# A memset and a wait behind each row scatter in a two-layer attention and mixture-of-experts kernel

## The chip, the core and the metric
The kernel runs on one core of a Trainium2 chip. The metric is the device time of one execution in microseconds (us). TensorE does matrix products, VectorE (DVE in the profile) and ScalarE (ACT) elementwise work, GpSimd (POOL) some elementwise work and the DMAs whose addresses come from a table of indices, SyncE (SP) issues the other DMAs.

## What is computed
Eight sequences of 256 tokens with 256 features go through two blocks. The first has attention with 16 heads and a small feed-forward layer that picks one of 8 low-rank updates per token. The second has causal attention with 16 query heads over 4 key groups, then a mixture of 32 experts, four per token, and one shared expert. The part around the change is the last:

```python
logits = flat @ router_w.T
scores = jnp.sqrt(jax.nn.softplus(logits))
_, idx = jax.lax.top_k(scores + expert_bias, K)        # K = 4 of E = 32
...
def body(acc, xs):
    wg, wu, wd, p = xs
    return (acc + p[:, None] * _clamped_swiglu(flat, wg, wu, wd), None)
```

## The kernel before
The 2048 tokens are 16 tiles of 128, two per sequence. The second attention goes through the sequences b = 0 to 7 and in each through 16 heads (a head step is b * 16 + head). TensorE computes scores into a ring of three banks, ScalarE exponentiates them (line 1162), TensorE multiplies by the values, VectorE divides (`divide`), adds to x and takes row statistics.

When a sequence has been divided, GpSimd computes the scale of its rows (`scale_rows`, lines 917 and 918), ScalarE normalizes the rows with it (`normalize_row`, line 1100), TensorE turns them and computes the logits, VectorE picks four experts for each token (`top_four`, `pick_four`), TensorE counts ranks within the experts (`ranks`) and VectorE turns them into row numbers (`find_slots`, line 2175; semaphore `slots_ready`). This goes by batches of sequences, `BATCHES = ((0, 2), (2, 2), (4, 2), (6, 1), (7, 1))`, each a first sequence and a count.

The rows are then sorted by expert in DRAM (`rows_by_expert`, 2048 rows for each expert): GpSimd issues 64 indirect DMAs, one for each tile t and pick k (`scatter`, line 922), each of which writes 128 rows of 260 floats. Its queue is in program order:
- During sequences 4 to 7, `scatter_nth` issues the scatters of batches 0 and 1 and five of batch 2, each behind a wait for its slots and for the exponential of a given head step. In each of these sequences `scale_rows(b - 1)` stands at head 8, in the same queue.
- Behind the attention come two more scatters of batch 2, a wait for the last division, two more, `scale_rows(7)`, the last seven of batch 2, picks 3 and 2 of batch 3 (four scatters), and then twelve: picks 3 and 2 of batch 4 (the last sequence), pick 1 of batches 3 and 4, pick 0 of batches 3 and 4.

Meanwhile VectorE works out which blocks of 128 rows belong to which expert, and SyncE loads blocks (`load_block`, line 761) from `rows_by_expert` for TensorE, which turns each (line 1720) and multiplies it by its expert's weights (1731, 1742). The first eight blocks wait for levels of the semaphore `picks_placed`: a token's picks are in order of expert number, so expert 0's rows are all in pick 3 (level 1), expert 1's in picks 3 and 2 (level 2), all others need all 64 scatters (level 3, which GpSimd sends itself when `placed[0]` says that the last have landed). Expert 0 has 338 rows here (three blocks), expert 1 has 411 (four). There are 80 block steps. Results go back by rank through 80 more indirect DMAs of GpSimd (line 982).

Of the kernel before, what the change touches and what calls it, by code (L numbers as in the profile page):

```python
# [16 lines left out]
P = 128  # L17
# [10 lines left out]
QT = SEQ // P  # L28
# [13 lines left out]
TAG = 16384.0  # L42
MASKED = -1.0e30
BLOCKS = -(-(TOKENS * TOPK + EXPERTS * (P - 1)) // P)
TURNS = 8
BLOCKS += -BLOCKS % TURNS
FEWEST = TOKENS * TOPK // P // TURNS
LEADING = 2 * TILES // TURNS + 1
FIRST = 8
# [113 lines left out]
BATCHES = ((0, 2), (2, 2), (4, 2), (6, 1), (7, 1))  # L163
# [73 lines left out]
def two_block_kernel(nc, x_in, wqkv0, wproj, bproj, wffn, debias, wdown, center, slope,  # L237
                     wqkv1, bq1, bk1, bv1, router, ebias, wexp_in, out):
    ctx = ExitStack()
    with ctx:  # L240
        def sb(name, shape, dt=F32):
            return ctx.enter_context(nc.sbuf_tensor(name, shape, dt))
# [4 lines left out]
        def cut(whole, start, size, shape=None, **axes):  # L247
            part = whole[:, start:start + size]
            return part.rearrange(shape, **axes) if shape else part
# [90 lines left out]
        work = cut(exps, 0, TILES * TOPK * EXPERTS, "p (t k e) -> p t k e", t=TILES, k=TOPK)  # L340
        SMALL = ONE_AT + (EXPERTS - 2) * EW
        most = max(size for _, size in BATCHES) * QT * EXPERTS
        lg, soft, ex, ln = (cut(arena, SMALL + i * most, most, tile_expert, t=most // EXPERTS) for i in range(4))
        sbi = cut(arena, SMALL + 2 * most, most, tile_expert, t=most // EXPERTS)
# [34 lines left out]
        sco = cut(arena, PICK_F + TOPK * te, te, tile_expert, t=TILES)  # L379
        trash = cut(arena, PICK_F + TOPK * te + te, BLOCKS)  # L380
        sg, se = (cut(attn_w, i * CHUNK, CHUNK) for i in (0, 2))
# [3 lines left out]
        wsh = cut(exps, P_RING * P_WIDTH[1], EW)  # L385
        tagb, pad, valid = (cut(exps, 4 * CHUNK + i * BLOCKS, BLOCKS) for i in range(3))
        experts = cut(arena, ONE_AT, EXPERTS * EW)
# [9 lines left out]
        goes = sb("goes", [P, 4], U32)  # L397
        vec = sb("vec", [P, 12])
        zero = sb("zero", [P, XW])
        before = sb("before", [P, P], BF16)  # L400
        onesb = sb("onesb", [P, P], BF16)
        m8 = cut(ffn_w, 0, TILES * 8, "p (t e) -> p t e", t=TILES)
# [12 lines left out]
        slot = cut(bpb, 2 * EXPERTS, TILES * TOPK).bitcast(U32).rearrange("p (t k) -> p t k", t=TILES)  # L415
        eb_i = sb("eb_i", [1, BLOCKS], I32)
        start_i = sb("start_i", [1, BLOCKS], I32)
        first_i = sb("first_i", [1, 2 * FIRST], I32)
# [14 lines left out]
        xs = nc.dram_tensor("rows_by_expert", [EXPERTS * TOKENS, XW], F32, kind="Internal").ap()  # L433
        ys = nc.dram_tensor("results_by_rank", [TOKENS * TOPK + BLOCKS * P, D], F32, kind="Internal").ap()

# [112 lines left out]
        def block_trips(eng):  # L548

            eng.wait_ge(blocks_ready, 2)  # L550
            return eng.value_load(trips_i[0:1, 1:2], min_val=0, max_val=BLOCKS // TURNS - FEWEST) + FEWEST

# [81 lines left out]
        def _(sp):  # L634
# [117 lines left out]
            def starts_of(first, size):  # L752
                return nc.values_load_multi_w_load_instructions(
                    start_i[0:1, bass.ds(first, size)],
                    engines=[mybir.EngineType.SP], min_val=0, max_val=EXPERTS * TOKENS - P,
                    skip_runtime_bounds_check_because="a block's first row lies in its expert's rows")[1]
# [16 lines left out]
            trips = block_trips(sp)  # L773
            with sp.Fori(FIRST // TURNS, trips) as i:
                starts = starts_of(TURNS * i, TURNS)
                for j in range(TURNS):
# [24 lines left out]
        def _(pool):  # L801
# [29 lines left out]
            def then(ins):  # L831

                pool_steps[0] += 1
                ins.then_inc(pool_step, 1)
                pool.wait_ge(pool_step, pool_steps[0])
# [84 lines left out]
            def scatter(t, k):  # L920

                pool.indirect_dma_start(xs, bass.IndirectOffsetOnAxis(ap=slot[:, t, k:k + 1], axis=0),  # L922
                                        xn4[:, t, :], None).then_inc(placed[max(k - 1, 0)], 16)

            def scatter_nth(j, n, after):
                pool.wait_ge(slots_ready, j + 1)
                pool.wait_ge(exp_ready[1], after + 1)
                t, k = divmod(n, TOPK)
                scatter(BATCHES[j][0] * QT + t, k)

            def scatter_picks(j, picks):

                pool.wait_ge(slots_ready, j + 1)
                first, size = BATCHES[j]
                for k in picks:
                    for t in range(first * QT, (first + size) * QT):
                        scatter(t, k)
# [20 lines left out]
            for t, k in tiles[:2]:  # L958
                scatter(t, k)
# [839 lines left out]
        def _(dve):  # L1799
# [280 lines left out]
            def pair(n, b, k):  # L2080
                count = b * len(PAIRS[n]) + k
                src = pair_bank[count % 2]
                dve.wait_ge(unit_ready[n], count + 1)
                (qt, h0, nh, nk), (_, h1, _, _) = PAIRS[n][k]
                if n == 0:
                    out = mx[b % 2][:, :, h0:h0 + nh]
                    ins = dve.tensor_reduce(out, src.rearrange("p (q h k) -> p q h k", q=QT, k=nk), AX.X, ALU.max)  # L2087
                else:
                    out = mx[b % 2][:, qt, h0:h0 + 2 * nh]
                    ins = dve.tensor_reduce(out, src.rearrange("p (h k) -> p h k", k=nk), AX.X, ALU.max)  # L2090
                ins.then_inc(unit_done[n], 1)
                if k == len(PAIRS[n]) - 1:
                    dve.wait_ge(unit_done[n], count + 1)
                    if b:
                        dve.wait_ge(negT_ready[n], b)
                    step(n, dve.tensor_scalar(neg[:, :, 0, :], mx[b % 2][:, :, :], -1.0, None, ALU.mult))
                    dve.scalar_tensor_tensor(out=neg[:, :, 1, :], in0=mx[b % 2][:, :, :], scalar=-1.0, in1=neg[:, :, 0, :],
                                             op0=ALU.mult, op1=ALU.subtract).then_inc(neg_ready[n], 1)
# [335 lines left out]
```

## Time and profile before

| what | us |
|---|---|
| median of 3 runs | 607.91 |
| lowest, highest | 606.37, 610.05 |
| span of the profiled execution, first to last instruction | 624.5 |
| TensorE busy | 550.5 (88%) |
| VectorE busy | 433.0 (69%) |
| ScalarE busy | 346.5 (55%) |
| GpSimd busy | 241.2 (39%) |
| GpSimd in the 64 scatters | 63.2 |
| GpSimd idle just before them | 57.6 |

The profile is that of another execution than the timed ones. Its own device time isn't recorded apart from the span; it can only be longer than the span. The span is 16.6 us above the median. A row of the timeline gives start, duration, engine, line and operation, and in brackets the idle time of the engine before it and what ended it.

### The profile page before, as it was taken

The page shows a single profiled execution, that of the slowest core. Times are in us where ns is not written, and L with a number is a line of the kernel's source. Part 1 is how long each engine was busy: PE and PEld are TensorE (multiplying, and loading weights), DVE is VectorE, ACT ScalarE, POOL GpSimd, SP SyncE. Part 2 cuts the span into 40 slices and gives each one's busy share as a digit, 9 for nine tenths or more (in the row PEclk, how much of TensorE's full clock was granted, in tenths as well). Part 3 has the DMA queues.
Part 4 walks back from the last instruction along what each step waited for, and adds up shares of the span by engine and source line. Part 5 has one row for each costly group of instructions (what it writes and reads, how often), then busy time and mean ns, then how long its engine had stood idle before and what let it go on. Part 6 is the DMA issues. An engine that isn't in the chain of part 4 may idle for free.

```text
span 624.5 us, 14114 instructions
## 1 busy us (share of the span) xinstructions
PE 550.5 (88%) x4231; PEld 390.9 (63%) x4232; DVE 433.0 (69%) x1298; ACT 346.5 (55%) x898; POOL 241.2 (39%) x341
## 2 busy tenths in 40 slices
PE   9998799999879989989998888866589999989996
PEld 4665455665458754666666665534367787778775
DVE  5678858888147886677788683535667777778755
ACT  3533657776826578456675456513146565656672
POOL 2533000000153213266544435556735555555530
PEclk9999979999999999999999899778799999999998
DMA  8599707000680005766505162235545454445498
GB/s 252 179 304 331 211 1 207 3 3 3 192 219 1 2 1 166 209 206 183 229 19 206 62 229 71 70 137 219 170 126 140 140 159 144 151 135 154 143 396 328
DMA packets 49554, 95.24 MB, mean 153 GB/s; under 512 B 8596, under 2 KB 40540, under 8 KB 46940
## 3 DMA queue, kind: packets, MB, share of 16 engines
q1 hardware_dynamic: 41820, 75.34, 39.4%
q0 software_dynamic: 7680, 19.21, 8.2%
q8 instruction: 30, 0.49, 0.3%
q14 instruction: 24, 0.20, 0.1%
HBM read 58.54 MB, written 35.59 MB: 151 GB/s over the span
## 4 chain that ended last, share of the span: by engine, by line
PE 54%; DVE 20%; issue 9%; ACT 6%; DMA 4%; POOL 3%; another core or an unknown queue 2%; SPq 1%; DVEq 0%; ACTq 0%; POOLq 0%
PE banks L1731 7%; PE banks L1513 6%; PE banks L1469 5%; PE banks L1322 4%; PE banks L1742 4%; PE banks L1534 4%; DVE mx L2087 3%; DVE mx L2090 3%; PE banks L1399 3%; PE banks L1794 2%; PE banks L1328 2%; DMA arena<-negT 2%; PE banks L1720 2%; DMA pvs<-rows_by_expert 2%
## 5 line engine op out<-in xcount | busy, mean ns | idle before, releaser
L1162 ACT ACTIVATE arena<-banks 128x512 f32<-128x512 f32 (+1 forms) x256 | 130.1, 550 | 83.3 <-PE banks L1513 45.8
L982 POOL DMA_INDIRECT results_by_rank<-attn_w,goes x80 | 77.3, 966 | 72.2 <-issue 47.9
L1513 PE MATMUL banks<-arena 98*128 98x256 bf16 (+1 forms) x512 | 88.6, 267 | 15.9 <-DVE arena L2186 3.8
L2087 DVE TENSOR_REDUCE mx<-banks 128x4 f32<-128x1024 f32 x64 | 76.0, 1220 | 18.1 <-PE banks L1469 18.0
L922 POOL DMA_INDIRECT rows_by_expert<-arena,bpb x64 | 63.2, 987 | 57.6 <-ACT arena L1162 22.4
L1469 PE MATMUL banks<-arena 96*128 96x256 bf16 (+1 forms) x512 | 81.5, 263 | 4.2 <-DVE mx L2087 2.5
L1731 PE MATMUL banks<-arena,attn_w 128*128 x320 | 84.4, 387 | 0.3 <-issue 0.3
L1513 PEld LDWEIGHTS banks<-arena 98*128 98x128 bf16 x512 | 43.2, 100 | 49.7 <-ACT arena L1162 15.0
L2090 DVE TENSOR_REDUCE mx<-banks 128x4 f32<-128x1024 f32 (+1 forms) x48 | 57.7, 1221 | 22.3 <-PE banks L1473 20.2
L1469 PEld LDWEIGHTS banks<-arena 96*128 96x128 bf16 x512 | 49.9, 99 | 20.0 <-issue 6.0
L1731 PEld LDWEIGHTS banks<-arena,attn_w 128*128 128x128 f32 x320 | 55.6, 194 | 5.1 <-issue 0.7
L1742 PE MATMUL banks<-arena,attn_w 128*128 x160 | 49.0, 388 | 7.4 <-issue 4.1
L1235 ACT ACTIVATE attn_w<-attn_w 128x128 f32<-128x128 f32 x80 | 24.8, 310 | 53.3 <-DVE attn_w L2285 40.0
L2285 DVE TENSOR_SCALAR attn_w<-banks 128x256 f32<-128x256 f32 x80 | 34.0, 424 | 24.8 <-PE banks L1731 12.3
L848 POOL DMA_DIRECT2D arena<-negT x24 | 12.1, 509 | 99.5 <-ACT negT L1084 99.5
L1473 PE MATMUL banks<-mask_s,identb 128*128 128x128 bf16 x256 | 40.3, 221 | 0.5 <-issue 0.5
L1742 PEld LDWEIGHTS banks<-arena,attn_w 128*128 128x128 f32 x160 | 28.8, 189 | 16.5 <-issue 12.8
L1720 PE MATMUL banks<-ident,pvs 128*128 128x128 f32 x160 | 31.7, 281 | 7.7 <-DMA pvs<-rows_by_expert 7.7
L1534 PE MATMUL banks<-arena 128*17 128x256 f32 x512 | 34.7, 389 | 1.1 <-ACT pvs L1093 1.1
L944 POOL TENSOR_SCALAR_AFFINE_SELECT arena<-arena 128x256 f32<-128x256 f32 x64 | 26.0, 418 | 21.2 <-ACT arena L1162 21.1
L1241 ACT ACTIVATE attn_w<-banks 128x256 f32<-128x256 f32 x80 | 31.0, 387 | 2.8 <-DMA results_by_rank<-attn_w,goes 2.5
L840 POOL TENSOR_TENSOR arena<-arena 128x512 bf16<-128x512 f32 x16 | 18.2, 1160 | 37.1 <-ACT arena L994 37.1
(253 smaller groups left out, 1095.7 us busy)
## 6 DMA issues: line engine op xcount, KB each, us to landing
arena<-parts_dram SPq DMA_DIRECT2D x72, 256.0 KB, 4.1
pvs<-rows_by_expert SPq DMA_DIRECT2D x80, 130.0 KB
parts_dram<-arena SPq DMA_DIRECT2D x24, 384.0 KB, 4.8
arena<-results_by_rank SPq DMA_DIRECT2D x6, 1024.0 KB, 10.3
arena<-in SPq DMA_DIRECT2D x2, 2304.0 KB
rows_by_expert<-zero SPq DMA_DIRECT2D x1, 4160.0 KB, 23.6
arena<-in SPq DMA_DIRECT2D x2, 1920.0 KB
arena<-in SPq DMA_DIRECT2D x3, 768.0 KB
```

The source lines that it names most:

```text
L922: pool.indirect_dma_start(xs, bass.IndirectOffsetOnAxis(ap=slot[:, t, k:k + 1], axis=0), xn4[:, t, :], None).then_inc(placed[max(k - 1, 0) ...
L982: pool.indirect_dma_start(ys, bass.IndirectOffsetOnAxis(ap=goes[:, j % 4:j % 4 + 1], axis=0), yb[j % 4], None).then_inc(y_stored[j % 4], 16)
L1162: act.activation(p_ring[n][:, i % P_RING, :], st_bank[RING_AT[n]["s", b, s] % 3][:, 0:P_WIDTH[n]], ACT.Exp, scale=HD ** -0.5).then_inc(exp ...
L1469: ins = pe.matmul(dst[:, a * nk:(a + 1) * nk], q_rows(n, slice(0, STACK), h0 + a, b, qt * P, P), k_rows(n, slice(0, STACK), h0 + a, b, 0, ...
L1473: ins = pe.matmul(dst[:, a * nk + nk - P:(a + 1) * nk], identb[:, :], mask_s[:, :], start=False, stop=True)
L1513: ins = pe.matmul(dst[:, at:at + SEQ - q0], keys, q_rows(n, slice(0, ROWS), s, b, q0, SEQ - q0), start=True, stop=(n == 0 or b < POOL_MASKS))
L1534: ins = pe.matmul(pv_bank[rows, col:col + SEQ], vals, p[:, kt * SEQ:(kt + 1) * SEQ], start=(kt == 0), stop=(kt == QT - 1))
L1720: ins = pe.transpose(bank[p][:, k * P:(k + 1) * P], xb[:, q, k * P:(k + 1) * P], ident[:, :])
L1731: ins = pe.matmul(bank[2 + p][:, 0:2 * INNER], xbT[:, p, k, :], experts[:, bass.ds(e * EW + k * 2 * INNER, 2 * INNER)], start=(k == 0), st ...
L1742: pe.matmul(bank[6 + p][:, 0:D], hidT[:, p, :], experts[:, bass.ds(e * EW + 2 * KD * INNER, D)], start=True, stop=True).then_inc(y_ready, 1)
L2087: ins = dve.tensor_reduce(out, src.rearrange("p (q h k) -> p q h k", q=QT, k=nk), AX.X, ALU.max)
L2090: ins = dve.tensor_reduce(out, src.rearrange("p (h k) -> p h k", k=nk), AX.X, ALU.max)
```

## The change
A tile `pause` of 128x256 floats is allocated. Behind each scatter whose tile t is below 14 (all but the last sequence's), GpSimd writes zeros to it, and `then` makes GpSimd wait until that memset has finished before it goes on. 56 of the 64 scatters are followed by it. Nothing reads the tile.

```diff
+PAUSE = 256
...
+        pause = sb("pause", [P, PAUSE])
...
                 pool.indirect_dma_start(xs, bass.IndirectOffsetOnAxis(ap=slot[:, t, k:k + 1], axis=0),
                                         xn4[:, t, :], None).then_inc(placed[max(k - 1, 0)], 16)
+                if t < BATCHES[4][0] * QT:
+                    then(pool.memset(pause[:, :], 0.0))
```

GpSimd's queue from the scatters in the heads of sequence 7 to the one behind the last division, before (L917 and L918 are the scaling of rows, `divided1` the last division):

```order
L922 DMA rows_by_expert<-arena,bpb 65536x260 [waits exp_ready1,slots_ready] x5
L922 DMA rows_by_expert<-arena,bpb 65536x260 x2
L922 DMA rows_by_expert<-arena,bpb 65536x260 [waits divided1]
L922 DMA rows_by_expert<-arena,bpb 65536x260
L917 TENSOR_TENSOR rstd<-var,mhalf 128x2 [waits rows_var]
```

The same place now, from the fourth of the five on (numbers of the queue in front, lines are two or more higher):

```order
196 L924 DMA rows_by_expert<-arena,bpb 65536x260 [waits exp_ready1,slots_ready,pool_step]
197 L927 MEMSET pause 128x256
198 L924 DMA rows_by_expert<-arena,bpb 65536x260 [waits exp_ready1,slots_ready,pool_step]
199 L927 MEMSET pause 128x256
200 L924 DMA rows_by_expert<-arena,bpb 65536x260 [waits pool_step]
201 L927 MEMSET pause 128x256
202 L924 DMA rows_by_expert<-arena,bpb 65536x260 [waits pool_step]
203 L927 MEMSET pause 128x256
204 L924 DMA rows_by_expert<-arena,bpb 65536x260 [waits divided1,pool_step]
205 L927 MEMSET pause 128x256
206 L924 DMA rows_by_expert<-arena,bpb 65536x260 [waits pool_step]
207 L927 MEMSET pause 128x256
```

The order of the scatters is the same; each next one waits for `pool_step`, the memset's semaphore, and the scaling of the last rows stands behind nine memsets counted from the first of the five.

The last twelve scatters on GpSimd, before:

```order
L922 DMA rows_by_expert<-arena,bpb 65536x260 [waits slots_ready]
L922 DMA rows_by_expert<-arena,bpb 65536x260 x3
L922 DMA rows_by_expert<-arena,bpb 65536x260 [waits slots_ready]
L922 DMA rows_by_expert<-arena,bpb 65536x260
L922 DMA rows_by_expert<-arena,bpb 65536x260 [waits slots_ready]
L922 DMA rows_by_expert<-arena,bpb 65536x260
```

And now (the first row is the last sequence's first scatter):

```order
232 L924 DMA rows_by_expert<-arena,bpb 65536x260 [waits slots_ready,pool_step]
233 L924 DMA rows_by_expert<-arena,bpb 65536x260 x3
234 L924 DMA rows_by_expert<-arena,bpb 65536x260 [waits slots_ready]
235 L927 MEMSET pause 128x256
236 L924 DMA rows_by_expert<-arena,bpb 65536x260 [waits pool_step]
237 L927 MEMSET pause 128x256
238 L924 DMA rows_by_expert<-arena,bpb 65536x260 [waits slots_ready,pool_step]
239 L924 DMA rows_by_expert<-arena,bpb 65536x260
```

Two memsets stand between picks 1 of batch 3 and those of batch 4; the same pattern follows once more for pick 0, so four of the twelve are followed by one.

## Rows read from the trace of the kernel before

**Rows 1.** The page of the profile, its first line.
```profile
span 624.5 us, 14114 instructions
```

**Rows 2.** Busy us (instructions) by stretch: PE, PEld, DVE, ACT, POOL; clock, DMA share, GB/s.
```profile
400.00:425.00 25.00, 17.86 (x140) 11.43 (x139) 10.87 (x37) 9.65 (x23) 14.02 (x17) 0.86 0.41 149
425.00:450.00 25.00, 14.10 (x73) 8.34 (x72) 16.97 (x67) 4.84 (x10) 16.97 (x18) 0.80 0.51 175
...
500.00:525.00 25.00, 23.70 (x129) 19.78 (x127) 18.71 (x94) 14.67 (x57) 13.88 (x15) 1.00 0.53 154
```

**Rows 3.** Timelines of TensorE, ScalarE, TensorE, VectorE: start, us, engine, line, operation.
```profile
406.30 0.22 PE L1516 MATMUL banks<-mask_t,identb 128*128 128x128 bf16 x1
...
411.02 0.49 ACT L1162 ACTIVATE arena<-banks 128x384 f32<-128x384 f32 x1 [5.77 <-remote]
...
432.48 0.21 PE L1591 MATMUL banks<-products,onesb 128*128 128x32 bf16 x1
...
436.36 0.22 DVE L2167 SCALAR_TENSOR_TENSOR arena<-iota,banks 128x64 f32<-128x64 f32 x1 [3.63 <-remote]
```

**Rows 4.** The chain that ended last, SyncE's part: start, us, what.
```profile
443.24 0.74 SPq L747
...
444.19 0.04 SPq L768
...
445.64 0.68 SPq L761
...
454.86 0.03 SPq L768
...
455.14 2.06 DMA pvs<-rows_by_expert
```

**Rows 5.** Timeline of TensorE, the transpositions of blocks 4 and 7.
```profile
457.24 0.44 PE L1720 MATMUL banks<-ident,pvs 128*128 128x128 f32 x2 [0.44 <-DMA pvs<-rows_by_expert]
...
462.17 0.38 PE L1720 MATMUL banks<-ident,pvs 128*128 128x128 f32 x2
```

**Rows 6.** Timeline of GpSimd, 371 to 453 us: scatters (L922) and scalings.
```profile
371.41 0.96 POOL L922 DMA_INDIRECT rows_by_expert<-arena,bpb  x1 [7.80 <-DVE bpb L2175]
...
378.70 1.04 POOL L922 DMA_INDIRECT rows_by_expert<-arena,bpb  x1 [0.52 <-issue]
...
386.89 0.96 POOL L922 DMA_INDIRECT rows_by_expert<-arena,bpb  x1 [2.43 <-ACT arena L1162]
...
399.70 0.72 POOL L917 TENSOR_TENSOR rstd<-var,mhalf 128x2 f32<-128x2 f32 x1
...
402.50 1.04 POOL L922 DMA_INDIRECT rows_by_expert<-arena,bpb  x1 [1.80 <-ACT arena L1162]
...
416.90 1.28 POOL L922 DMA_INDIRECT rows_by_expert<-arena,bpb  x1 [5.80 <-DVE arena L2191]
418.49 0.96 POOL L922 DMA_INDIRECT rows_by_expert<-arena,bpb  x1 [0.31 <-issue]
419.48 0.73 POOL L917 TENSOR_TENSOR rstd<-var,mhalf 128x2 f32<-128x2 f32 x1
420.28 0.19 POOL L918 TENSOR_TENSOR shift<-nmean,rstd 128x2 f32<-128x2 f32 x1
420.64 1.04 POOL L922 DMA_INDIRECT rows_by_expert<-arena,bpb  x1 [0.16 <-issue]
...
437.98 0.96 POOL L922 DMA_INDIRECT rows_by_expert<-arena,bpb  x1 [3.15 <-DVE bpb L2175]
...
452.18 0.96 POOL L922 DMA_INDIRECT rows_by_expert<-arena,bpb  x1 [0.30 <-issue]
```

**Rows 7.** DMA activity, 454 to 455 us, in 40 slices (0.025 us each, tenths).
```profile
DMA  8440000000000000000000000000000000000000
```

**Rows 8.** Line 809, GpSimd's memset of a tile of nearly the same size.
```profile
L809 POOL MEMSET zero<- x1: 336/336/336, 1.6 to 1.6; 128x260 f32 x1
```

**Rows 9.** Timeline of ScalarE: the normalization that waits for the scaling at 399.70.
```profile
400.73 0.60 ACT L1100 ACTIVATE arena<-arena,shift,rstd 128x256 f32<-128x256 f32 x1 [0.77 <-POOL shift L918]
```

## The prediction
> **What bounds the kernel now.** I read the busy shares in windows of 25 us first, then the chain that ended last where TensorE idles, then the timelines of the engines on both sides of each idle piece. TensorE works nearly all the time in the expert loop (23.70 of 25 us), but only 17.86 and 14.10 of 25 us between 400 and 450 us [rows 2]. This stretch, from the end of the second attention to the first expert blocks, is the one that the change touches, so its chain decides.
>
> Two odd things are to be seen in it. One: TensorE starts its last score matmul at 406.30 (0.22 us), and ScalarE, idle and waiting for it, starts at 411.02; what ended its 5.77 us of idle time is given as "remote", which is nobody on this core [rows 3]. An ordinary hand-over leaves about 0.1 us, so some 4.4 us are unexplained. TensorE's rank matmul ends at 432.69, idle VectorE takes the ranks at 436.36: another 3.6 us [rows 3]. Two: behind the instruction at 444.19 SyncE's register instructions, 0.04 us each before, take about 0.68 us each; at 454.86 they are back at 0.03 [rows 4]. All of these lie where GpSimd issues scatters every 1.26 us without a break (0.96 us of work, 0.30 us between) [rows 6]. And the rate behind them: from block 4 on TensorE runs at (462.17 - 457.24) / 3 = 1.64 us a block [rows 5], so whatever delays the early blocks passes to the end unreduced.
>
> Block 7 is the first whose expert is number 2 (the inputs give experts 0 and 1 three and four blocks), and its load waits for level 3, which is all 64 scatters landed. The last scatter starts at 452.18 and the packets in the software queue end 0.1 us into the window from 454 [rows 6, 7]: 1.9 us from start to landing. From a load's start to its first transposition it is 457.24 - 455.14 = 2.1 us [rows 4, 5].
>
> **What is the profile's own.** The span is 624.5 us [rows 1], 16.6 above the median of 607.91, and what lies around a span would only add to that. The loop runs at TensorE's own rate, so the surplus isn't spread evenly; it must sit in idle time, and the unexplained idle time lies in these 50 us. Take both stalls out and let SyncE's instructions cost 0.04: all of the last batch's work comes 8.0 us earlier, and SyncE takes up the blocks at 443.24 - 8.0 = 435.2 [rows 4]. The first load goes out about 1.2 us after that (0.74 for the table and a dozen instructions at 0.04), and block 7 would be on TensorE at 436.4 + 2.1 + 7 x 1.64 = 450.0. GpSimd's side allows it: with the first stall gone (the second isn't on its way) its last twelve scatters could start at 430.7, or at 437.98 less the two stalls, 430.0, if the slots came last; the last of them starts 452.18 - 437.98 = 14.2 later, at 444.9 [rows 6], and 444.9 + 1.9 + 2.1 = 448.9. So block 7 moves from 462.17 to 450.0, and 624.5 - 12.2 = 612.3 is near the timed runs. I therefore take it as likely that timed runs don't have these stalls.
>
> That rests on rows; a page points the same way. The Trainium skill ("NOTIFIC — the notification-queue block", section 3, Interfaces) says that trace records leave through a block that can hold back the engines that write them when an internal FIFO fills. No run here shows that block. By it a pause would mend the profile and not the timed run.
>
> **The change, part by part.** It adds 56 memsets of 128x256 and 56 waits, behind each of the 64 scatters but the last sequence's 8; it removes and moves nothing else. The allocation of a tile costs no time.
> - One memset: the nearest row is the 128x260 one, 336 ns [rows 8]; I take 0.34.
> - Its wait and what follows: a GpSimd instruction behind a scatter starts after 0.03 (419.45 to 419.48), one behind its own wait after 0.07; the scatter that follows a compute instruction starts after 0.16 where it waits for nothing, 0.52 where it also names exp_ready and slots_ready, and takes 1.04 instead of 0.96 [rows 6].
> - So the spacing of scatters that are all ready goes from 1.26 to 1.04 + 0.03 + 0.34 + 0.07 + 0.52, about 2.03, in the head-by-head part, and to 1.68 in the tail. The low bound for both has the short gap and the short scatter: 0.96 + 0.03 + 0.34 + 0.08 + 0.17, about 1.60. Below that nothing is possible, since the memset can't start before the scatter ends nor the next scatter before the memset does.
>
> GpSimd is idle before many scatters, waiting for the exponential or the slots that gate them, and this hides the pauses as long as a gate comes later than the queue. It no longer does from batch 1 on. With 2.03: four scatters from 371.41, then the fifth sequence's scaling, the next scatter at 380.5 instead of 378.70; twelve of them take 11 x 2.03, and the scaling of sequence 6's rows starts at 404.3 instead of 399.70 [rows 6]. ScalarE already waits 0.77 us for that scaling [rows 9], so its next exponentials start up to 4.6 later, and TensorE behind them. Seven more scatters follow from 405.9, the one that waits for the last division comes at 419.0 (before: 416.90), the last scaling at 422.2 (before: 419.48), the eleven scatters from 423.4 take 11 x 1.68 = 18.5, and the last twelve start at 441.8, later than their slots. Four of these twelve have a pause (0.42 each), so the last starts at 441.8 + 14.2 + 1.7 = 457.7, and block 7 is on TensorE at 457.7 + 1.9 + 2.1 = 461.7. With 1.60 the gates at 386.89 and 402.50 still hold; the last scaling then starts at 416.7, the last twelve scatters at 435.5, the last one at 451.0, and block 7 is at 455.0.
>
> The point is that GpSimd becomes the bound, and that its chain hardly asks whether the stalls exist: 455.0 to 461.7 either way. The result depends on what it is compared with.
>
> **Likeliest: the stalls are the profiler's.** Against 450.0, block 7 comes 5.0 (short spacing) to 11.7 us (long) later. The long price needs the 0.52 gap behind every head-by-head memset, and I have that gap only behind the scalings; neither end is nearer to a row of a memset in this place, so I take the middle, 8.4: 607.9 + 8.4 = 616.3. Own range 612.9 to 619.6. Chance 0.58.
>
> **Rival 1, faster: the stalls are real and pauses cure them.** For it: the two stalls and the slow instructions all lie in runs of scatters 1.26 apart, and the expert loop, whose scatters come one a block, 1.64 apart, keeps TensorE busy for 23.70 of 25 us [rows 2]. Against it: the surplus of the span then has no place. Against 462.17 the change gives 461.7 to 455.0, so 0.5 to 7.1 us less: 600.8 to 607.4. By interpolation between the two ends it passes 3 us when the spacing stays under about 1.85 us. Chance 0.27, somewhat over half of it beyond 3 us.
>
> **Rival 2, no change: the stalls are real and stay.** The pauses leave as many scatters and descriptors as before, so the change may not do what it is named for. The division then ends as late as now or later (421.2 with the long spacing: 416.90 plus ScalarE's delay), and the last scatter starts 1.8 to 3.6 later than computed above. Block 7 lies between -3.5 and +1.3 of 462.17: 604.4 to 609.2. Chance 0.15.
>
> **How the numbers follow.** 0.5%, or 3 us, is about what a measurement of this kernel can tell from no change. Faster by more: over half of rival 1, 0.17. Within: the rest of rival 1 and nearly all of rival 2, with a little of the likeliest case's low end, 0.22. Slower: 0.61. The range goes from 603.0, which leaves out the lower part of rival 1 (about 0.1), to 621.0, a little above the long price because delays of ScalarE could also reach TensorE on a way I haven't priced.
>
> **What would show it.** In the profile after: scatters in the tail 1.60 to 1.70 apart, in the head-by-head part up to 2.03; ScalarE's wait for the scaling at about 400 us grown from 0.77 to over 3 us (or hardly grown, if spacing is short); no GpSimd wait for the last slots, where 3.15 us stood; the last scatter's start between 451 and 458. The span would change little in the likeliest case and the timed runs grow: profiled and timed would come closer together. If the "unknown queue" pieces vanish and the timed runs fall as well, rival 1 is right. The forecast is wrong if the timed runs really contain the stalls, or if level 3 isn't what block 7 waits for.

## The result

The changed kernel takes 616.65 us (median of 6 runs, 613.66 to 619.74), the kernel before 607.14 us (median of 6 runs, 603.41 to 610.14). The ratio is 1.019, 95% interval 1.016 to 1.022: about 11.5 us slower. The profiled execution of the changed kernel took 616.09 us. The forecast was 616.3. Here and below, a run over 1.5% above the fastest of its kernel is left out of the ratios: one of the kernel before at 1075.31 us, one at 614.95 us (4 columns, waited for) and one at 614.79 us (heads, scaling first).

The page of the changed kernel: its span (answers to [rows 1]) and the group of the scatters, now on L924: busy us, mean ns of one, idle us before them and what ended most of it.

```profile
span 614.3 us, 14180 instructions
...
L924 POOL DMA_INDIRECT rows_by_expert<-arena,bpb x64 | 63.3, 990 | 35.9 <-ACT arena L1166 13.2
```

Busy time by stretch, as in [rows 2]: us (instructions) of PE, PEld, DVE, ACT, POOL; granted clock, DMA share, GB/s.

```profile
400.00:425.00 25.00, 18.03 (x108) 10.71 (x109) 11.40 (x44) 9.77 (x24) 20.75 (x32) 0.81 0.55 201
425.00:450.00 25.00, 19.38 (x103) 13.99 (x102) 19.20 (x80) 6.08 (x19) 19.89 (x26) 0.85 0.52 160
...
500.00:525.00 25.00, 23.08 (x124) 18.88 (x124) 18.43 (x88) 14.33 (x55) 12.74 (x15) 1.00 0.48 143
```

TensorE still idles in the same 50 us, and the expert loop runs at its old rate. The stalls of 4.4 and 3.6 us [rows 3] and SyncE's instructions of 0.68 us [rows 4] are gone from this trace. That doesn't make the pause their cure: the first experiment finds them gone without any pause.

GpSimd's timeline, to be held against [rows 6]: start us, us, engine, line, operation, and in brackets the idle time before it with what ended it.

```profile
397.28 0.72 POOL L919 TENSOR_TENSOR rstd<-var,mhalf 128x2 f32<-128x2 f32 x1
398.07 0.19 POOL L920 TENSOR_TENSOR shift<-nmean,rstd 128x2 f32<-128x2 f32 x1
400.06 1.04 POOL L924 DMA_INDIRECT rows_by_expert<-arena,bpb  x1 [1.80 <-ACT arena L1166]
...
401.72 0.97 POOL L924 DMA_INDIRECT rows_by_expert<-arena,bpb  x1 [0.28 <-ACT arena L1166]
402.69 0.33 POOL L927 MEMSET pause<- 128x256 f32 x1
403.29 0.97 POOL L924 DMA_INDIRECT rows_by_expert<-arena,bpb  x1 [0.28 <-POOL pause L927]
...
414.38 0.72 POOL L919 TENSOR_TENSOR rstd<-var,mhalf 128x2 f32<-128x2 f32 x1
...
448.62 0.96 POOL L924 DMA_INDIRECT rows_by_expert<-arena,bpb  x1 [0.30 <-issue]
```

A pause of zeros takes 0.33 us and starts the moment its scatter's work ends; the next scatter follows 0.28 us behind it. The spacing is 403.29 - 401.72 = 1.57 us, in the head-by-head part and in the tail alike; without a pause it is 1.26 (0.96 of work and a gap of 0.30). So a pause costs 0.31 us where scatters are ready, and from 400.06 to 448.62 no gap between its instructions is longer than 0.30 us.

Who waits for the scalings: ScalarE's normalizations of the rows of sequences 6 and 7 (answers to [rows 9]).

```profile
398.30 0.60 ACT L1104 ACTIVATE arena<-arena,shift,rstd 128x256 f32<-128x256 f32 x1 [4.32 <-POOL shift L920]
...
415.40 1.09 ACT L1104 ACTIVATE arena<-arena,shift,rstd 128x256 f32<-128x256 f32 x2 [8.46 <-POOL shift L920]
```

And behind the second one TensorE, with a transposition, the logits and an attention output product:

```profile
416.64 1.09 PE L1566 MATMUL banks<-ident,arena 128*128 128x128 f32 x4 [4.73 <-ACT arena L1104]
418.50 1.89 PE L1577 MATMUL banks<-wr,arena 128*128 128x32 f32 x8 [0.78 <-ACT arena L1109]
...
420.95 3.76 PE L1625 MATMUL banks<-arena 128*128 128x512 f32 x4
```

At the end of the stretch, SyncE's waits between 400 and 470 us (us in total, times, longest), and the chain of work that ended last, from the load of block 7 at 452.04 on (start, us, what; [rows 4] has its like):

```profile
SPq L763 <- POOLq L977: 2.3, 1, 2.3
```

```profile
452.04 0.33 SPq L763
...
454.08 2.09 DMA pvs<-rows_by_expert
```

SyncE waits 2.3 us for GpSimd's word that all scatters have landed (level 3), loads block 7 at 452.04, reads the table of the further blocks and loads block 8 at 454.08. The last scatter had started at 448.62. So here the load of block 7 waits for GpSimd's queue, as forecast.

### The profile page after: what moved, and what is told of

Its sections match the earlier page's. It is cut to its first block and busy times, and to the rows that moved or that the text cites. A ratio compares the mean times of both kernels' runs of the same rounds, so it can differ in the third digit from the quotient of the medians.

```text
span 614.3 us, 14180 instructions
## 1 busy us (share of the span) xinstructions
PE 549.8 (89%) x4231; PEld 392.6 (64%) x4232; DVE 434.1 (71%) x1298; ACT 345.7 (56%) x898; POOL 259.8 (42%) x397
## 5 line engine op out<-in xcount | busy, mean ns | idle before, releaser
L924 POOL DMA_INDIRECT rows_by_expert<-arena,bpb x64 | 63.3, 990 | 35.9 <-ACT arena L1166 13.2
L1517 PEld LDWEIGHTS banks<-arena 98*128 98x128 bf16 x512 | 43.7, 101 | 47.9 <-ACT arena L1166 14.0
```

The source lines that it names most:

```text
L1517: ins = pe.matmul(dst[:, at:at + SEQ - q0], keys, q_rows(n, slice(0, ROWS), s, b, q0, SEQ - q0), start=True, stop=(n == 0 or b < POOL_MASKS))
```

## The experiments

All times below but the changed kernel's own (6 runs against 6, as above) are compared with 19 to 35 runs of the kernel before on the same chip, median 605.5 to 606.1 us; differences in us are what the ratio has over 1, times 605.5. Two slips stand in some of the expectations as recorded: 53 pauses where there are 56, and 37 behind the first scatter of batch 1 where there are 40.

To compare traces, all positions in the table are counted from the start of the first scatter of batch 1 (in the traces 365 to 376 us; it waits for its slots, 6.4 to 7.3 us idle before it, in every kernel). "Block 9" is TensorE's transposition of the first block that runs freely behind level 3 and SyncE's table. Each position is read from one trace. In four kernels whose times don't differ measurably (before, earlier gates, batch 0 only, 4 columns without a wait) block 9 lies between +81.0 and +81.4; a fifth, 4 columns waited for, has +83.3.

| kernel | ratio, 95% interval | us | scaling of seq. 7 | last scatter | block 9 |
|---|---|---|---|---|---|
| before, once more | 0.998 (0.996 to 1.001) | -1.0 | +40.0 | +69.8 | +81.3 |
| changed | 1.019 (1.016 to 1.022) | +11.4 | +44.8 | +79.0 | +89.9 |
| heads only, 37 pauses | 1.010 (1.006 to 1.015) | +6.3 | +43.7 | +73.7 | +87.8 |
| tail only, 19 | 1.008 (1.004 to 1.012) | +4.9 | +40.8 | +75.0 | +88.2 |
| not in the last twelve, 52 | 1.013 (1.009 to 1.018) | +8.0 | +45.4 | +79.0 | +89.8 |
| batch 1 only, 16 | 1.004 (1.001 to 1.007) | +2.4 | +41.1 | +71.6 | +83.0 |
| batch 0 only, 16 | 1.002 (0.999 to 1.006) | +1.3 | +39.2 | +69.1 | +81.0 |
| 4 columns, waited for, 56 | 1.000 (0.998 to 1.003) | +0.2 | +41.2 | +72.2 | +83.3 |
| earlier gates, none | 1.001 (0.998 to 1.003) | +0.3 | +40.3 | +70.1 | +81.3 |
| scaling first, 56 | 1.015 (1.008 to 1.022) | +9.1 | +40.5 | +77.7 | +89.1 |
| heads, scaling first, 37 | 1.006 (1.002 to 1.011) | +3.9 | +40.3 | +72.8 | +83.9 |
| two writings each, 56 | 1.057 (1.048 to 1.067) | +34.8 | +56.7 | +96.9 | +107.2 |
| 4 columns, no wait, 56 | 1.000 (0.997 to 1.004) | +0.1 | +39.3 | +69.7 | +81.4 |

What lies ahead of batch 1 is not in this count. From the first scatter of batch 0 to the first of batch 1 the traces have 33.6 us in the kernel before, 36.0 in the changed one, 43.2 with two writings each, and 33.6 to 35.9 in the others.

Two readings were set against each other. **Theory 1**: GpSimd's queue up to the last scatter sets the end of the stretch, and the pauses are summed there. **Theory 2**: the pauses ahead of a scaling delay ScalarE and TensorE, and that delay runs to the end on their own path.

### The kernel before, once more

No edit.

> The kernel before, unchanged, profiled once more. If the two stalls and the slow SyncE instructions of the first profile are a rare event (or the profiler's own), this profile has a span near the timed runs (about 605 us), no idle piece of ScalarE over 3 us that ends with nobody on this core near 406 us, block 7 on TensorE near 445 to 450 us, and GpSimd waits about as long for the last slots as before. If they belong to scatters 1.26 us apart, they are here again and the span is near 624 us. Time: 607 us, ratio 1.00.

The profiled execution has a span of 607.9 us, not 624.5. GpSimd, ScalarE and TensorE where [rows 3, 6] had the stalls:

```profile
span 607.9 us, 14114 instructions
```

```profile
412.73 0.73 POOL L917 TENSOR_TENSOR rstd<-var,mhalf 128x2 f32<-128x2 f32 x1
...
413.89 1.04 POOL L922 DMA_INDIRECT rows_by_expert<-arena,bpb  x1 [0.16 <-issue]
...
442.51 0.96 POOL L922 DMA_INDIRECT rows_by_expert<-arena,bpb  x1 [0.30 <-issue]
```

```profile
398.20 0.60 ACT L1100 ACTIVATE arena<-arena,shift,rstd 128x256 f32<-128x256 f32 x1 [3.05 <-POOL shift L918]
...
413.77 1.09 ACT L1100 ACTIVATE arena<-arena,shift,rstd 128x256 f32<-128x256 f32 x2 [5.33 <-POOL shift L918]
```

```profile
408.91 5.97 PE L1621 MATMUL banks<-arena 128*128 128x512 f32 x12
415.00 0.63 PE L1562 MATMUL banks<-ident,arena 128*128 128x128 f32 x4
416.42 1.05 PE L1573 MATMUL banks<-wr,arena 128*128 128x32 f32 x8 [0.78 <-ACT arena L1105]
...
417.71 1.96 PE L1621 MATMUL banks<-arena 128*128 128x512 f32 x4
```

No idle time ended by "remote" is in it, and no slow SyncE instruction, though its scatters run 1.26 us apart without a break from 413.89 to 442.51. In both of these traces (spans 607.9 and 614.3 us) the run's own time is 1.7 to 1.8 us over the span, and the spans recorded for the timed executions stand in the same relation to their times. So timed and profiled executions are recorded alike, and the first profile was one long execution: its span alone lies above every timed run of the kernel before listed here (601.1 to 610.7) but the one of 1075.31 us, which has no trace. Long single executions thus occur in timed runs too. Dense scatters alone don't cause the stalls, and "the profiler's own" is not supported either. What held the engines up there is open.

This trace also shows what bounds the ordinary kernel. TensorE runs from 408.91 to 414.88 on an attention output product and goes straight on with the transposition at 415.00; the normalization had been there since 414.86. In the chain that ended last, GpSimd doesn't occur between 400 and 456 us. But its queue is nearly full (three waits behind 397 us, 1.94, 0.72 and 1.00 us, none for the last sequence's slots) and close to a tie: in the trace of the last kernel of the table, as fast as this one, ScalarE's normalization is 1.0 us late for TensorE and the chain does go over GpSimd up to the last scaling. At the other end, the last scatter starts at 442.51, block 7's load goes at 445.96, and TensorE takes block 7 without a wait.

### Pauses in one part only

Heads only: the pauses behind the 37 scatters issued inside the attention. Tail only: behind the 19 of the tail.

```
-                if t < BATCHES[4][0] * QT:
+                if t < BATCHES[4][0] * QT and paused[0]:
```

where `paused[0]` is set to False (heads) or True (tail) ahead of the first scatter of `tiles`.

> Pauses only behind the 37 scatters issued head by head; none in the tail. Theory 1 (the loss is the length of GpSimd's queue up to the last scatter, level 3): the pauses here cost what the gates don't hide, that is the delay of sequence 6's scaling and what ScalarE loses by waiting for it, about 3 us: 610 us. Theory 2 (the loss is ScalarE and TensorE waiting for the scaling of rows, the tail is hidden behind the first seven blocks): nearly the whole loss is here, 614 to 616 us.

> Pauses only behind the 19 scatters of the tail outside the last sequence, none head by head. Theory 1: 19 pauses of 0.31 us (1.57 against 1.26) less what the wait for the last division and the slots hides, about 5 to 6 us: 612 to 613 us. Theory 2: little, 607 to 609 us.

They cost 6.3 us (interval 3.6 to 8.9) and 4.9 us (2.7 to 7.1), together about what the change costs (11.4), and the last scatter is 3.9 and 5.2 us later, together about the 9.2 of the change. The time of the heads lies between the two forecasts, about 3 us and 7 to 9; that of the tail fits theory 1 and not theory 2. The traces show two different ways. The chain that ended last of the heads-only kernel, in the part before the last sequence's routing:

```profile
407.53 0.96 POOL rows_by_expert L926
408.49 0.34 POOL pause L929
...
413.19 0.96 POOL rows_by_expert L926
414.17 0.91 POOL rstd L919
415.38 1.10 ACT arena L1107 x2
416.61 1.10 PE banks L1569 x4
```

GpSimd's scatters and pauses lead to the scaling at 414.17, this to ScalarE's normalization, and this to TensorE; from there on the chain is TensorE, VectorE and ScalarE again, and block 9 comes 6.5 us late although the last scatter is only 3.9 late. That is theory 2. In the tail-only kernel the last scaling, ahead of which only four of its pauses stand, is 0.8 us late; SyncE waits 2.3 us for level 3. That is theory 1. Its trace has two further oddities: block 8's load took 4.30 us instead of 2.1 to 3.5, and TensorE, after two idle pieces, ran slowly (last section). So its block 9 is late by more than its measured median.

### No pause among the last twelve scatters

`paused[0] = False` ahead of the last twelve; four of them had a pause.

> As the change, but without the four pauses among the last twelve scatters. Theory 1 (block 7 waits for level 3, the last scatter landed): these four are worth 4 x 0.31 = 1.2 us in full: 615.4 us. Theory 2 (blocks wait for SyncE's own instructions or for an earlier level): no difference from the change, 616.6 us.

+8.0 us against +11.4, intervals 5.4 to 10.7 and 9.7 to 13.2. They overlap, so what the four cost (1.2 by the count) isn't resolved; in the two profiles the last scatter starts at the same place, +79.0, because this one's last scaling came 0.6 us later and several of its scatters ran long (up to 1.40 us).

### Where in the heads

Pauses behind batch 1's scatters alone, then behind batch 0's alone.

```
-                if t < BATCHES[4][0] * QT:
+                if BATCHES[1][0] * QT <= t < BATCHES[2][0] * QT:
```

```
-                if t < BATCHES[4][0] * QT:
+                if t < BATCHES[1][0] * QT:
```

> Pauses only behind the 16 scatters of batch 1, the ones whose gates lie around the scaling of sequence 6's rows; 48 scatters are left as in the kernel before. Theory 1 (GpSimd's queue is full from about the first scatter of batch 1 on, so each pause there delays the scaling of sequence 6's rows and the last scatter by its own 0.31 us): 16 x 0.31 = 5.0 us at most, +4 to +5 us, and the scaling of sequence 6 about 3 us later than in the kernel before, counted from the first scatter of batch 1. Rival (every pause ahead of the tail costs the same, 6.3 us over 37 pauses, 0.17 us each, wherever it stands): 16 x 0.17 = +2.7 us.

> Pauses only behind the 16 scatters of batch 0, which wait for their gates far apart. Theory 1: GpSimd waits for each gate anyway, the pause lies inside that wait: within 0.5 us of the kernel before. Rival (0.17 us for each pause ahead of the tail): +2.7 us.

Batch 0 costs nothing that can be measured (-0.8 to +3.4 us), and its trace has everything behind batch 1's first scatter within 0.8 us of the old place, on the early side: its 16 pauses lie ahead of the 6.4 us for which GpSimd still waits for batch 1's slots. Ahead of that scatter its trace is 0.7 us longer than that of the kernel before. Batch 1 costs +2.4 us (0.5 to 4.2), half of what theory 1 gave it. By the times alone the rival, +2.7 us for each batch, would fit both intervals; what speaks against it are the traces. In batch 1's trace the scaling of sequence 6 is 2.6 us late (+27.1 against +24.5), but the last one 1.1 and block 9 1.7: unpaused scatters and a gate behind the first scaling take the rest back. So by the traces a pause has no fixed price. The two batches together make 3.7 us by their medians, and 2.6 of the heads' 6.3 are left for the five pauses of batch 2, which stand right ahead of the last scaling; these differences are within the intervals.

### Earlier gates, without any pause

```
-SCATTERS = ((68, 13, 8, 16), (99, 11, 8, 16), (122, 9, 8, 5))
+SCATTERS = ((68, 13, 8, 16), (99, 8, 8, 16), (120, 4, 8, 5))
```

> The kernel before without any pause, with the gates of batches 1 and 2 moved earlier: 8 scatters of batch 1 in 8 attention heads instead of 11, and 5 of batch 2 from head 120 in steps of half a head. Theory 1 (the queue of GpSimd up to the last scatter is what the end of the kernel waits for, and it stands idle at gates before it is full): 1 to 2 us of idle time between gates is taken out, last scatter and time 1 to 3 us earlier. Rival (the rows' scaling, which stands at a fixed place of the queue, comes later by the scatters that are now ahead of it, and ScalarE and TensorE wait for it): no gain or up to 2 us slower.

No gain can be seen: +0.3 us (-1.2 to +1.8). The scaling of sequence 6 does come 1.9 us earlier (+22.6 against +24.5), but nothing on TensorE does: block 9 stays at +81.3. This fits the chain above: in that trace of the kernel before GpSimd isn't the bound, so filling its gaps brings nothing.

### The writing or the wait

The pause with 4 columns and its wait; then 4 columns of its own for each scatter and no wait.

```
-PAUSE = 256
+PAUSE = 4
```

```
-                    then(pool.memset(pause[:, :], 0.0))
+                    pool.memset(pause[:, 4 * pauses[0]:4 * pauses[0] + 4], 0.0)
+                    pauses[0] += 1
```

> All 53 pauses as in the changed kernel, with their wait, but the zeros are 4 columns wide instead of 256. Theory W (the length of the writing sets the price: 0.33 us of it and a gap of 0.28 us take the place of a gap of 0.30 us): with a writing of about 0.05 us the spacing of scatters is about 1.30 us instead of 1.57, and the time +1 to +2 us against the kernel before. Rival (the wait for the writing sets the price, whatever its length): spacing near 1.57 us and about +11 us as with 256 columns.

> Behind each of the 53 scatters a writing of 4 columns, each into columns of its own, and no wait for it. With the wait the 4 columns cost 0.10 us a scatter (spacing 1.36 us: 0.96, 0.12 and a gap of 0.28 us). Theory (the gap of 0.28 us is the scatter's own start, the same 0.30 us that stands between two scatters without a pause): spacing stays 1.36 to 1.38 us. Rival (the gap is the wait for the writing to end): it falls away or shrinks to 0.1 us, spacing 1.26 us or less. The time is within 0.3% of the kernel before either way.

The first of these rows are from the kernel with the wait, the others from the one without.

```profile
400.97 0.96 POOL L924 DMA_INDIRECT rows_by_expert<-arena,bpb  x1 [0.28 <-POOL pause L927]
401.94 0.12 POOL L927 MEMSET pause<- 128x4 f32 x1
402.33 0.96 POOL L924 DMA_INDIRECT rows_by_expert<-arena,bpb  x1 [0.28 <-POOL pause L927]
```

```profile
398.05 0.97 POOL L926 DMA_INDIRECT rows_by_expert<-arena,bpb  x1 [0.20 <-issue]
399.02 0.12 POOL L929 MEMSET pause<- 128x4 f32 x1
399.32 0.97 POOL L926 DMA_INDIRECT rows_by_expert<-arena,bpb  x1 [0.19 <-issue]
```

With the wait: 0.96 + 0.12 + 0.28 = 1.36 us, and a time that doesn't differ from before (-1.5 to +1.9 us), so theory W holds and its rival (1.57 us, +11 us) is out; the short writing takes 0.12 us, not 0.05. Without the wait: 0.97 + 0.12 + 0.19, 1.28, so the writing lies inside the 0.30 us that stand between two scatters anyway. The recorded theory for the last kernel, that the gap belongs to the scatter, is wrong; the rival is nearer. The wait gives up the cover, some 0.1 us, and then further writing counts in full: 0.21 us more of it (0.12 to 0.33) makes the spacing 0.21 us longer (1.36 to 1.57). Whether a writing of 256 columns without a wait would be covered was not run.

### Two writings

```
                     then(pool.memset(pause[:, :], 0.0))
+                    then(pool.memset(pause[:, :], 0.0))
```

> Behind each of the 53 scatters two writings of 128x256 zeros with a wait each. Each pause grows by 0.33 us of writing and a small gap, from 0.31 to about 0.70 us, spacing from 1.57 to about 1.95 us. Theory (GpSimd's queue is full from the gates on): 37 paused scatters behind the first of batch 1 x 0.70 = 25.9 us, less some 2.5 us that gates take in, +22 to +26 us. Rival (what is lost is lost once, by falling out of step with the gates): +12 to +15 us.

```profile
400.75 0.97 POOL L924 DMA_INDIRECT rows_by_expert<-arena,bpb  x1 [0.45 <-POOL pause L928]
...
402.86 0.96 POOL L924 DMA_INDIRECT rows_by_expert<-arena,bpb  x1 [0.45 <-POOL pause L928]
...
424.60 0.96 POOL L924 DMA_INDIRECT rows_by_expert<-arena,bpb  x1 [0.28 <-POOL pause L928]
...
426.57 0.96 POOL L924 DMA_INDIRECT rows_by_expert<-arena,bpb  x1 [0.28 <-POOL pause L928]
```

The spacing is 2.11 us in the heads and 1.97 around the tail's start, later 1.94: a pause of 0.7 to 0.85 us. The gap before the scatter is 0.45 us where it also names `exp_ready` and `slots_ready`, 0.42 where it names one further semaphore and 0.28 where it names none; in the changed kernel 0.28 stands before nearly all of them, and no run tells why it differs. The last scatter is 27.1 us late, 34.8 are lost. The rival, a loss that comes once, is out; my 22 to 26 was too low, for the pauses counted were 37 and not 40, the gap is longer, and the pauses of batch 0 are no longer hidden. Ahead of batch 1's first scatter this trace is 43.2 - 33.6 = 9.6 us longer, where ScalarE waits for the scaling of sequence 4's rows and TensorE 5.6 us for ScalarE:

```profile
362.67 0.60 ACT L1105 ACTIVATE arena<-arena,shift,rstd 128x256 f32<-128x256 f32 x1 [6.12 <-POOL shift L920]
```

Block 9 comes 25.9 us late in the count from batch 1, and with these 9.6 that is 35.5, close to the 34.8 lost.

### The scaling two scatters earlier

In the changed kernel the inputs of the two last scalings were there at 393.93 and 409.76, and GpSimd came to them at 397.28 and 414.38. Here both stand two scatters earlier, with all 56 pauses, and then with those of the heads only.

```
-                    if h == ROWS_VAR:
+                    if h == ROWS_VAR - 2 * (b == SEQS - 1):
...
+            scale_rows(7)
             pool.wait_ge(divided[1], SEQS * QT)
             for t, k in tiles[2:4]:
                 scatter(t, k)
-            scale_rows(7)
```

> The changed kernel with all 53 pauses, but the scaling factors of sequences 6 and 7 stand two scatters earlier in GpSimd's queue. In the changed kernel their inputs were ready 3.4 and 4.6 us before GpSimd came to them, so the factors of sequence 7 should come about 3 us earlier than +44.8 us (counted from the first scatter of batch 1), while the sum of GpSimd's work is the same. Theory 1 (with pauses in the tail, the queue up to the last scatter sets the time): last scatter stays at +79 us and the time within 1.5 us of the changed kernel, +10 to +12 us against the kernel before. Theory 2 (TensorE's own work behind the late scaling sets it): 3 us are won back, +7.5 to +8.5 us.

> The same early scaling, with the 37 pauses ahead of the tail only and none in the tail. Here the last scatter was 3.9 us late and TensorE's expert blocks 5 to 6 us, from block 0 on. Theory 2: the factors' lateness is what makes block 0 late, so +6.3 us shrinks to +2.5 to +3.5 us. Theory 1 (the queue alone counts): the last scatter stays 3.9 us late and +5 to +6.5 us remain.

With all pauses the scaling of sequence 7 comes 4.3 us earlier, the last scatter 1.3 and block 9 only 0.8: SyncE waits 2.5 us for level 3, and that hangs on the queue's sum. Measured are +9.1 us with an interval of 4.8 to 13.3, which by itself decides nothing; the trace speaks for theory 1. With the pauses of the heads only, the same edit moves the scaling by 3.4 us and block 9 by 3.9, and the loss falls from 6.3 to 3.9 us (1.3 to 6.5); the two intervals overlap, so the times don't decide, and the traces speak for theory 2. Of the heads-only kernel the slowest of 4 runs was profiled and of this one nearly the fastest of 10; the count from batch 1 takes out what differs ahead of it. So, by the traces, both hold, each for its kernel: late scalings cost time while the tail is free, and as soon as the tail is paused too, the queue's end covers them.

## Why the prediction held

- **That the stalls aren't in timed runs** decided the sign, and was right: apart from the one at 1075.31 us no run of the kernel before is above 610.7. The reason given for it, the profiler's own, is not supported: thirteen other profiled executions don't have them. The argument from the surplus of the span was sound; it says that this execution was unlike the timed ones, not why. Of the 16.6 us between its span and that of the kernel before, once more, 13.5 lie ahead of block 7 and 3.1 behind it; the prediction put 12.2 ahead of it.
- **The spacing** was given as 2.03 (heads) and 1.68 us (tail), low bound 1.60. It is 1.57 in both. The memset was right (0.34 against 0.33); mis-sized were the gaps. I had taken 0.03 ahead of it and 0.07 to 0.08 behind its wait, where there is nothing ahead and 0.28 in all up to the scatter. The gap of 0.52 and the 1.04 us stay with scatters behind a scaling or a gate, as [rows 6] had them; behind a memset there is 0.28. Choosing the middle between the ends was too much: the low end was closer.
- **The path through ScalarE** was right. The wait for the scaling of sequence 6's rows, 0.77 us in [rows 9], is 4.32 in the changed kernel ("over 3 us"), though in the ordinary execution before it is 3.05 already; the one for sequence 7's went from 5.33 to 8.46. TensorE waits 4.73 us for the normalization behind this second one and 0.97 for that behind the first. The prediction followed the first and gave no separate price to the second.
- **The queue as the new bound** was right: level 3 gates block 7, last scatter at 448.62. The forecast for it was 451.0 to 457.7, for block 7 455.0 to 461.7; it is at 454.21. They are 2.4 and 0.8 us below the low ends; in this execution the first scatter of batch 1 also started 1.8 us earlier than in the first profile (369.63 against 371.41).
- **From the last scatter's start to the load** I took 1.9 us. Where SyncE waits for it, it is 452.04 - 448.62 = 3.4. The 1.9 was the end of packets in the queue; the word of it goes over GpSimd's two waits and a third instruction to SyncE.
- **The kernel before without stalls** was put at block 7 = 450.0. An ordinary execution has it at 448.70, and in it the wait of 3.15 us for the last slots [rows 6] isn't there either. So "no GpSimd wait for the last slots" wasn't a mark of the change.
- **The sum**: 8.4 us from the middle of the ends, 11.4 measured (9.7 to 13.2). Counted from the first scatter of batch 1, the traces give 9.2 us up to the last scatter (4.8 up to the last scaling, 15 x 0.31 behind it, less rounding and long scatters), 8.6 up to block 9 and 9.5 up to the end; in these two traces the stretch from the first scatter of batch 0 to that of batch 1 adds 36.0 - 33.6 = 2.4. Whether these 2.4 us belong to batch 0's pauses is open: four other kernels with the same 16 pauses have 0.7 there, the heads-only kernel 2.3, and the kernel with batch 1's pauses only 1.3. With the low spacing I would have forecast 5.0. The hit of 616.3 is thus partly luck: a spacing too long was offset by a hand-over too short (1.9 against 3.4) and by a block 7 of the kernel before put too late (450.0 against 448.70).
- **The chances** don't quite add up. Neither rival reaches 3 us slower, so "slower" could be no more than the 0.58 of the likeliest case, and "within" no less than about 0.25; 0.61 and 0.22 were given.
- **The rivals.** Rival 1 needed stalls that are caused by dense scatters. The reading behind it was not exact: the second stall lasts until 436.36, but [rows 6] have GpSimd idle for the 3.15 us before 437.98. The kernel before run again has the dense scatters and no stall, and its timed runs are the faster ones. Rival 2 falls with it. "The span would change little, the timed runs grow" was half right: the span fell by 10 us against the odd one, and grew by 6.4 us against an ordinary one.

## What to carry to other kernels

Take a second profile before reading a stall of several microseconds as part of the kernel: hold the span against the timed runs, and where it lies well above them, read that trace for its order and durations, not for its gaps. A short instruction between two DMA issues of GpSimd was free here when nobody waited for it (0.12 us in a gap of 0.30); waited for, it cost nearly its length (0.10 of 0.12 us, 0.31 of 0.33), and on an in-order queue the cost is passed on to whatever stands behind it: here the small scalings of rows and, at the end, the word that all scatters have landed. It stays hidden only while the queue has a longer wait behind it: 16 pauses of 0.31 us ahead of one of 7 us cost nothing measurable, 16 of about 0.85 us cost time. When a queue's delay is to be priced, follow each instruction in it that somebody else waits for, and add the last link (end of transfers to the waiter's start) from a row that shows the waiter.

## What was not expected of the hardware

**An idle TensorE paid twice.** In the changed kernel TensorE idled 4.73 us for the last normalization, and then three groups took 1.09, 1.89 and 3.76 us for 4, 8 and 4 matmuls. In the kernel before, once more, there was no such wait, and the same groups took 0.63, 1.05 and 1.96 us. The granted clock by stretches of 5 us in both, the changed kernel first (columns as above):

```profile
415.00:420.00 5.00, 2.58 (x12) 2.24 (x13) 0.00 (x0) 3.36 (x6) 4.20 (x8) 0.54 0.89 354
420.00:425.00 5.00, 5.00 (x22) 2.63 (x23) 3.72 (x14) 2.31 (x5) 3.94 (x7) 0.50 0.23 81
```

```profile
415.00:420.00 5.00, 3.89 (x30) 2.38 (x30) 3.67 (x17) 3.71 (x9) 3.84 (x4) 1.00 0.98 386
420.00:425.00 5.00, 2.63 (x31) 2.10 (x32) 4.76 (x18) 0.73 (x1) 3.79 (x4) 1.00 0.57 217
```

After the idle piece the clock is at 0.54 and 0.50, the lower of its two levels (1.2 against 2.4 GHz), which makes (1.09 - 0.63) + (1.89 - 1.05) + (3.76 - 1.96) = 3.1 us more work, part of it on the path of the last sequence's routing. The same stood in every trace with such a wait: idle 3.61 us, logits in 1.89 us (heads only); 4.17 and 1.89 (not in the last twelve); 3.16 and 1.81 (scaling first); 5.48 and 1.89 (two writings). Where the wait was 1.44 us or less the logits took 1.05 (eight traces). The length of the idle piece alone doesn't decide, though: in one of these eight (heads, scaling first; idle 0.95 us, then 0.78) the group behind the logits took 3.48 us instead of 1.96, at a clock of 0.59 from 410 to 412.5 us, and with idle pieces of 0.97 and 0.78 (4 columns, no wait) it took 1.96. The lower clock is a likely part of how a delay of 3.7 us at the scaling became 5 to 6.5 us at the blocks. The tail-only trace has it once more: after idle pieces of 1.16 and 2.45 us ahead of blocks 7 and 8,

```profile
452.10 0.44 PE L1727 MATMUL banks<-ident,pvs 128*128 128x128 f32 x2 [2.45 <-DMA pvs<-rows_by_expert]
...
454.42 1.22 PE L1749 MATMUL banks<-arena,attn_w 128*128 x2 [0.88 <-issue]
...
456.07 1.91 PE L1738 MATMUL banks<-arena,attn_w 128*128 x4
```

```profile
455.00:460.00 5.00, 5.00 (x16) 4.07 (x15) 1.38 (x7) 2.01 (x7) 0.99 (x2) 0.50 0.28 80
460.00:465.00 5.00, 5.00 (x29) 4.27 (x29) 3.81 (x20) 2.94 (x12) 2.04 (x3) 1.00 0.40 114
```

blocks 9 and 10 ran 3.2 us apart instead of 1.64. The kernel before pays it too: behind an idle piece of 3.96 us its first blocks run at a clock of 0.50, from 435 to 440 us.

**A long single execution.** One profiled execution of the kernel before had engines standing 4.4 and 3.6 us with nobody on the core to release them, and SyncE's register instructions at 0.68 instead of 0.04 us. None of the thirteen later traces has it. What it is, no run here tells, and no experiment but the second profile was aimed at it, since it didn't come again. The same trace has two shorter pieces of this kind, 1.73 us on ScalarE and 1.90 us on VectorE, ended at 344.89 and 345.73 us, where GpSimd has gaps of 0.66 and 1.91 us between its scatters.
